# Key and value biases written by ACT instead of multiplied in by PE, in a fused attention and FP4 layer

## The reference

```
q, k = elu(x @ Wq + bq) + 1, elu(x @ Wk + bk) + 1      # 16 heads of 16 columns
v    = x @ Wv + bv
k    = k / sqrt(sum(k*k per head) + 1e-6)
attn = (q @ k^T) @ v                                    # no softmax, no mask
y    = layernorm(x + attn @ Wo + bo) * gamma + beta     # eps 1e-6
x1   = layernorm(x + y)                                 # eps 1e-5
out  = layernorm(x1 + ffn(x1))                          # silu(gate) * up, then down
```

## Time and profile before

| | before |
|---|---|
| median of 3 runs | 707.12 us (707.09 to 709.07) |
| profiled execution: its time | 708.65 us |
| profiled execution: span | 706.9 us |
| mean granted clock of PE | 0.994 |
| PE busy | 687.4 us, 97% |
| DVE busy | 593.9 us, 84% |
| ACT busy | 485.0 us, 69% |
| POOL busy | 611.9 us, 87% |
| PE's share of the chain that ended last | 89% |
| bias products (L401) | 64 instructions, 18.1 us busy by their own lengths, which overlap |

### The profile page before, as it was taken

The page is one execution under the profiler, slowest core; times in us unless marked ns, Lnnn a source line. Parts: engine busy times, 40 slices in busy tenths (PEclk is TensorE's granted clock), DMA queues, the critical chain, the costliest instruction groups (busy, mean ns, idle before and its releaser), DMA issues.

```text
span 706.9 us, 14230 instructions
## 1 busy us (share of the span) xinstructions
PE 687.4 (97%) x4370; PEld 603.9 (85%) x4370; DVE 593.9 (84%) x1448; ACT 485.0 (69%) x943; POOL 611.9 (87%) x951
## 2 busy tenths in 40 slices
PE   7999999999988999999999999999999999999995
PEld 6887878778866799999999999999999999999995
DVE  5788888885878888898898898998998898998774
ACT  4666766766667767767767767767767767767664
POOL 2989888987998999988988988988988988989766
PEclk9999999999999999999999999999999999999999
DMA  9443343344322021111111111111111111100001
GB/s 280 170 136 134 128 135 123 113 165 152 118 91 90 30 62 45 61 46 46 56 65 46 60 46 46 53 68 46 61 46 46 52 69 46 60 17 16 16 32 45
DMA packets 22272, 55.05 MB, mean 78 GB/s; under 512 B 2547, under 2 KB 5557, under 8 KB 22197
## 3 DMA queue, kind: packets, MB, share of 16 engines
q1 hardware_dynamic: 21776, 54.01, 22.5%
q10 hardware_dynamic: 420, 0.13, 0.1%
HBM read 28.90 MB, written 25.17 MB: 76 GB/s over the span
## 4 chain that ended last, share of the span: by engine, by line
PE 89%; POOL 4%; issue 3%; DVE 2%; ACT 1%; DMA 1%; SPq 0%; POOLq 0%; DVEq 0%; ACTq 0%
PE banks L377 23%; PE banks L379 22%; PE banks L378 22%; PE banks L519 8%; PE banks L490 7%; PE banks L415 2%; PE banks L388 2%; PE banks L533 1%; PE banks L532 1%; PE banks L401 1%; PE banks L444 1%; DMA arena<-in_L_attn_x_dram 1%; POOL arena L1126 1%; PE banks L452 1%; POOL lnbuf L1111 0%
## 5 line engine op out<-in xcount | busy, mean ns | idle before, releaser
L377 PE MATMUL banks<-wgu_hi,actT_lo 128*128 128x512 f32 (+1 forms) x384 | 149.8, 390 | 1.6 <-DVE resid L790 1.3
L378 PE MATMUL banks<-wgu_lo,actT_hi 128*128 128x512 f32 (+1 forms) x384 | 144.0, 375 | 0.0
L379 PE MATMUL banks<-wgu_hi,actT_hi 128*128 128x512 f32 (+1 forms) x384 | 143.3, 373 | 0.0
L1126 POOL TENSOR_TENSOR arena<-arena 128x960 f32<-128x960 f16 (+2 forms) x68 | 115.1, 1693 | 0.0
L688 ACT ACTIVATE arena<-banks 128x512 f32<-128x512 f32 x64 | 38.4, 599 | 111.7 <-PE banks L379 111.5
L1102 POOL TENSOR_TENSOR arena<-arena 128x704 f32<-128x704 f32 x64 | 89.1, 1392 | 21.1 <-DVE arena L907 19.0
L377 PE MATMUL banks<-wd_hi,actT_lo 128*128 128x256 f32 x320 | 100.1, 313 | 0.0
L920 DVE TENSOR_TENSOR actT_lo<-banks,actT_hi 128x512 fp32r<-128x512 f32 (+1 forms) x132 | 85.6, 674 | 16.9 <-ACT actT_hi L674 16.2
L379 PE MATMUL banks<-wd_hi,actT_hi 128*128 128x256 f32 x320 | 90.3, 282 | 0.0
L378 PE MATMUL banks<-wd_lo,actT_hi 128*128 128x256 f32 x320 | 90.2, 282 | 0.0
L377 PEld LDWEIGHTS banks<-wgu_hi,actT_lo 128*128 128x128 f32 x384 | 72.5, 189 | 11.2 <-DVE resid L790 1.7
(11 more groups left out here) (126 smaller groups left out, 1932.8 us busy)
## 6 DMA issues: line engine op xcount, KB each, us to landing
xs<-x_plus_scratch SPq DMA_DIRECT2D x32, 512.0 KB, 3.3
x_plus_scratch<-xs SPq DMA_DIRECT2D x24, 512.0 KB, 2.9
arena<-in_L_attn_x_dram SPq DMA_DIRECT2D x32, 256.0 KB, 3.6
out_dram<-arena SPq DMA_DIRECT2D x32, 256.0 KB, 2.1
x_plus_scratch<-arena SPq DMA_DIRECT2D x8, 512.0 KB, 2.9
resid<-in_L_ffn_w_down_dram SPq DMA_DIRECT2D x1, 704.0 KB, 7.7
resid<-in_L_ffn_w_gate_dram SPq DMA_DIRECT2D x1, 640.0 KB, 8.1
resid<-in_L_ffn_w_up_dram SPq DMA_DIRECT2D x1, 640.0 KB, 9.5
```

The costliest lines, as they stand in the source:

```text
L377: nc.tensor.matmul(dst, sl, mh, start=(k == 0), stop=False, skip_group_check=shared)
L378: nc.tensor.matmul(dst, sh, ml, start=False, stop=False, skip_group_check=shared)
L379: last = nc.tensor.matmul(dst, sh, mh, start=False, stop=(ended and k == n - 1), skip_group_check=shared)
L1126: nc.gpsimd.tensor_tensor(blocks(va[:, (n + 1) % 2, a:b]), blocks(vqc[n % 2].bitcast(F16)[:, a:b]), each(s14[:, n % 2, a // BLK:b // BLK]) ...
```

## The change

ACT gets a new operation, `kv_biases(p)`: before kv_project(p) it copies one row that holds bk + 1 and bv (broadcast over 128 partitions, 512 columns) into both banks of pair p, for p = 2 to 23 (`filled`). The products of these pairs add onto it (`begun`, so the first has start=False), the bias product L401 is left out, and DVE's v_bias becomes a copy. It stands in ACT's step p-1, behind x_high (and kv_out_copy) and before k_seeds. PE waits for it before kv_project. Pairs 0, 1 and 24 to 31 stay as they are. The row needs one more load (bk, 128 KB, on SP's queue before the loads of pairs 2 and 3), once on ACT an addition of 1, and a tile of its own for bo.

The addition of the half in the rounding of weights goes from DVE (w_round) to ACT (w_f16_chunk), 11 times.

In the steps p of 4 to 23 that have no turns of weights and for which (p-2) mod 4 is over 0, kv_accumulate(p-2) moves from behind kv_project(p) to in front of it, right behind the turns of x. These are nine: 4, 5, 7, 11, 15, 17, 19, 20 and 21.

```diff
@@ -123,7 +124,8 @@
         vqb = [words(o, RN * (RW + 2) // 2).bitcast(U16).rearrange("p (r c) -> p r c", c=RW + 2) for o in (7808, 8303)]
 
         qr = words(9075, 512)
-        bv_b, bo_b = words(9587, D), words(9843, D)
+        bkv = words(9587, 2 * D)
+        bv_b = bkv[:, D:2 * D]
         vqc = [words(o, VW // 2) for o in (8947, 9587)]
 
         qe = words(10099, 512)
...
@@ -265,6 +268,10 @@
 
             return p - 1 if p <= MERGE else p
 
+        def filled(p):
+
+            return 2 <= p < MERGE
+
         def mo_bank(b):
             return Q_BANK if b < B - 1 else KV_BANK + 1
 
@@ -314,6 +321,7 @@
             sp.dma_start(wq_st, Wq.rearrange("(k p) n -> p k n", p=P)).then_inc(wq_in, 16)
             sp.dma_start(bo_b[:, :], bo.partition_broadcast(P)).then_inc(xb_in, 16)
             sp.dma_start(beta_b[:, :], beta.partition_broadcast(P)).then_inc(xb_in, 16)
+            sp.dma_start(bkv[:, 0:D], bk.partition_broadcast(P)).then_inc(bk_in, 16)
@@ -370,11 +378,11 @@
 
         @block.tensor
         def _(pe):
-            def split_product(dst, stat, mov, n, ended=True, shared=False):
+            def split_product(dst, stat, mov, n, begun=False, ended=True, shared=False):
 
                 for k in range(n):
                     (sh, sl), (mh, ml) = stat(k), mov(k)
-                    nc.tensor.matmul(dst, sl, mh, start=(k == 0), stop=False, skip_group_check=shared)
+                    nc.tensor.matmul(dst, sl, mh, start=(not begun and k == 0), stop=False, skip_group_check=shared)
                     nc.tensor.matmul(dst, sh, ml, start=False, stop=False, skip_group_check=shared)
                     last = nc.tensor.matmul(dst, sh, mh, start=False, stop=(ended and k == n - 1), skip_group_check=shared)
                 return last
@@ -393,13 +401,17 @@
                 pe.wait_ge(xT_lo_s, p + 1)
                 after(pe, k_feat, kv_read(p))
                 after(pe, v_s, kv_read(p))
+                if filled(p):
+                    pe.wait_ge(kv_bias, p - 1)
                 for jj in range(2):
                     bank = kv_banks(p) + jj
                     c = slice((p % PPB) * 2 * P + jj * P, (p % PPB) * 2 * P + (jj + 1) * P)
-                    split_product(ps[:, bank, :], lambda k: (xT_hi[:, k, c], xT_lo[:, k, c]),
-                                  lambda k: (wkv_hi[:, k, :], wkv_lo[:, k, :]), KT, ended=False, shared=True)
-                    last = nc.tensor.matmul(ps[:, bank, 0:D], rows[:, D:], rows[:, 0:D], start=False, stop=True,
-                                            skip_group_check=True)
+                    last = split_product(ps[:, bank, :], lambda k: (xT_hi[:, k, c], xT_lo[:, k, c]),
+                                         lambda k: (wkv_hi[:, k, :], wkv_lo[:, k, :]), KT, begun=filled(p), ended=filled(p),
+                                         shared=True)
+                    if not filled(p):
+                        last = nc.tensor.matmul(ps[:, bank, 0:D], rows[:, D:], rows[:, 0:D], start=False, stop=True,
+                                                skip_group_check=True)
                 last.then_inc(kv_ps, 1)
 
             def kv_accumulate(p):
@@ -457,6 +469,11 @@
                     if p - 1 in WG_STEP:
                         pe.wait_ge(wT_lo, WG_STEP[p - 1] + 1)
                     x_transpose(p + 1)
+
+
+                early = 4 <= p < MERGE and p not in WG_STEP and (p - 2) % PPB > 0
+                if early:
+                    kv_accumulate(p - 2)
                 if p == -1:
                     warm_up(6)
                 if p == 0:
@@ -467,7 +484,7 @@
                 if p in WG_STEP:
                     pe.wait_ge(xT_lo_s, p + 2)
                     weights_turn(WG_STEP[p])
-                if pair(p - 2):
+                if pair(p - 2) and not early:
                     kv_accumulate(p - 2)
                 if p == 1:
                     pe.wait_ge(watt_lo, 3)
@@ -579,6 +596,9 @@
                 act.wait_ge(w_scaled, c + 1)
                 after(act, w_deq, c - 1)
                 nc.scalar.activation(wqn[:, c % 2, :], halves(wy[:, c % 2, :]), ACT.Copy, scale=F16_ONE).then_inc(w_f16, 1)
+                act.wait_ge(w_f16, c + 1)
+                q = wqn[:, c % 2, :].bitcast(U16)
+                nc.scalar.activation(q, q, ACT.Copy, bias=ROUND_HALF).then_inc(w_half, 1)
 
             def weights_high(g):
                 act.wait_ge(wT_ps, g + 1)
@@ -606,6 +626,19 @@
                 after(act, k_feat, p)
                 b = kv_banks(p)
                 nc.scalar.activation(kexp, ps[:, b:b + 2, 0:D], ACT.Exp, bias=mone[:, :]).then_inc(k_exp, 1)
+
+            def kv_biases(p):
+
+                if p == 2:
+                    act.wait_ge(bk_in, 16)
+                    act.wait_ge(bv_in, 16)
+                    nc.scalar.activation(bkv[:, 0:D], bkv[:, 0:D], ACT.Copy, bias=1.0).then_inc(bk_one, 1)
+                    act.wait_ge(bk_one, 1)
+                act.wait_ge(k_feat, p - 1)
+                act.wait_ge(v_s, p - 1)
+                b = kv_banks(p)
+                nc.scalar.activation(ps[:, b:b + 2, :], bkv[:, :].unsqueeze(1).broadcast_to([P, 2, 2 * D]),
+                                     ACT.Copy).then_inc(kv_bias, 1)
 
             def k_squares(p):
                 act.wait_ge(k_feat, p + 1)
@@ -636,6 +669,8 @@
                     act.wait_ge(cols_set, 2)
                 if p >= 7 and (p - 7) % PPB == 0 and (p - 7) // PPB < B:
                     kv_out_copy((p - 7) // PPB)
+                if filled(p + 1):
+                    kv_biases(p + 1)
                 if pair(p - 1):
                     k_seeds(p - 1)
                 if pair(p - 2):
@@ -771,9 +806,7 @@
                 scales_of(wam[:, g], wsn[:, g], ws14[:, g], winv[:, g], w_nudged, w_scale_s, c + 1)
 
             def w_round(c):
-                dve.wait_ge(w_f16, c + 1)
                 q = wqn[:, c % 2, :].bitcast(U16)
-                nc.vector.tensor_scalar(q, q, ROUND_HALF, None, ALU.add).then_inc(w_half, 1)
                 dve.wait_ge(w_half, c + 1)
                 nc.vector.tensor_scalar(q, q, ROUND_MASK, None, ALU.bitwise_and).then_inc(w_rounded, 1)
 
@@ -803,8 +836,11 @@
             def v_bias(p):
                 after(dve, kv_acc, p - 2)
                 b = kv_banks(p)
-                nc.vector.tensor_tensor(vb[:, p % 3, :, :], ps[:, b:b + 2, D:2 * D],
-                                        bv_b[:, :].unsqueeze(1).broadcast_to([P, 2, D]), ALU.add).then_inc(v_s, 1)
+                if filled(p):
+                    nc.vector.tensor_copy(vb[:, p % 3, :, :], ps[:, b:b + 2, D:2 * D]).then_inc(v_s, 1)
+                else:
+                    nc.vector.tensor_tensor(vb[:, p % 3, :, :], ps[:, b:b + 2, D:2 * D],
+                                            bv_b[:, :].unsqueeze(1).broadcast_to([P, 2, D]), ALU.add).then_inc(v_s, 1)
 
             def k_sums(p):
                 dve.wait_ge(k_sq, p + 1)
```

More of the change, by code:

```diff
@@ L76, in build @@
         gamma_b = sb("gamma_b", [P, D])
+        bo_b = sb("bo_b", [P, D])
         bq_c, bq_neg, bq_one = (sb(n, [P, KT]) for n in ("bq_c", "bq_neg", "bq_one"))
@@ L173, in build @@
         G_BANK, U_BANK, GU_BANK, T_BANK, AT_BANK, DN_BANK = 6, 7, 0, 4, 2, (3, 1)
-        wk_in, wv_in, wq_in, wffn_in, rows_in, bv_in, bq_in, xb_in, late_in = (
-            sem(n) for n in ("wk_in", "wv_in", "wq_in", "wffn_in", "rows_in", "bv_in", "bq_in", "xb_in", "late_in"))
+        wk_in, wv_in, wq_in, wffn_in, rows_in, bv_in, bq_in, bk_in, xb_in, late_in = (
+            sem(n) for n in ("wk_in", "wv_in", "wq_in", "wffn_in", "rows_in", "bv_in", "bq_in", "bk_in", "xb_in", "late_in"))
         consts_set, small_set, cols_set, mask_s = sem("consts_set"), sem("small_set"), sem("cols_set"), sem("mask")
@@ L186, in build @@
         xT_ps, xT_hi_s, xT_lo_s = sem("xT_ps"), sem("xT_hi_done"), sem("xT_lo_done")
+        bk_one, kv_bias = sem("bk_one"), sem("kv_bias")
         kv_ps, k_exp, k_feat, v_s, k_sq, k_ssq, k_se, k_log, k_seed = (
```

## The result

The change makes the kernel slower: median 712.74 us (710.76 to 713.65, six runs) against 707.19 (706.96 to 709.07, six runs) for before, ratio 1.0067 with a 95% interval of 1.0053 to 1.0081. 705.7 was forecast, and the range ended at 709.0. The profiled execution took 712.61 us with a span of 710.7 and a mean granted clock of 0.996, against 708.65, 706.9 and 0.994: 4.0 us more, because the profile of before lay 1.5 over its median.

A forecast was written before the change was run, and what follows sets the result against it. PE was taken as the bound, with ACT and POOL limiting gains. Of 5.3 us off PE's list, 1.2 at the step 22 turn plus step 23's 0.24 remained: 707.12 - 1.4 = 705.7 us, range 702.7 to 709.0.

The forecast's parts named there:

- The bias products: On PE, 22 pairs: two products fewer each, 44 x 0.12 = 5.3 us off PE's list, the most to win.
- The write's own price: On ACT, one 1024-element write into two banks per step: 1.06 us, 0.96 of queue, bounds 0.90 and 1.27.
- rival B: ACT becomes the pacemaker in steps 2 to 22 if a write holds its queue 1.3: 709.5 us, chance 0.15.
- The start: First steps: newton(0) at 18.0 instead of 17.01, k_hat(2) and k_hat(3) 1.0 later.
- The early waits: PE waits for k_hat before the moved kv_accumulate: 0.8, 0.2, 0.5 in steps 4, 5, 7, about 1.3 in step 21.
- The early block: kv_accumulate ahead of kv_project in nine steps: the move itself wins 0, ends -0.3 and +1.8.
- the neighbour: A float32 block next to kv_accumulate might remove its 0.20 extra cost, 9 x 0.20 = 1.8; taken as 0.
- The step that failed: Weight turns in steps 8, 12, 16: DVE off the path otherwise, x_low(p+1) makes PE wait 0.3, 0.1, 0.1.
- Steps 8 to 18 win 11 x 0.24 = 2.6 less 0.5 of waits: PE's sum over these steps, from 0.1 late at step 8 to step 19 beginning 2.0 early.
- The forecast gain of 1.4: Whole kernel: the step 22 weight turn 1.2 earlier, held by POOL, and 0.24 from step 23; chance 0.45.
- The probability of 0.13 for slower: Chance of a measurement over 709.2 us, mostly from ACT becoming the pacemaker through a costlier write.
- the rivals: PE keeps most of its gain, chance 0.22; ACT becomes the pacemaker, 0.15; nothing reaches the end, 0.18.

The follow-up runs named there:

- e3: The changed kernel with key and value biases left out in pairs 2 to 23 (no ACT write, no PE product): ratio to before 0.9963.
- e12: The changed kernel with the write between k_exps and k_squares, from pair 3 on, and the last four weight turns one step later: ratio to before 0.9932.
- e4: The kernel before with only the nine kv_accumulate moved in front of kv_project: ratio to before 1.0005.
- e1: The changed kernel with kv_accumulate back behind kv_project in the nine steps: ratio to before 1.0065.
- e2: The changed kernel with the bias write moved behind k_seeds, ahead of q_maps and k_exps: ratio to before 1.0077.
- e14: The changed kernel with the bias write moved between q_maps and k_exps: ratio to before 1.0074.
- e5: The changed kernel with the bias write moved into ACT's wait between k_exps and k_squares: ratio to before 0.9970, median 706.54 us.
- e8: The changed kernel with the write between k_exps and k_squares, kv_accumulate back behind kv_project and the half back on DVE: ratio to before 0.9990.
- e9: The changed kernel with the half back on DVE: ratio to before 1.0060.
- e11: The changed kernel with the write between k_exps and k_squares and the last four weight turns one step later: ratio to before 0.9949.

## Why the prediction was wrong, step by step

**The bias products, right.** 44 products at 0.12; the product is left in 20 rows instead of 64, steps without a wait are 0.24 to 0.34 shorter, and in e3 and e12 they stay so.

**The write's own price, right.** 1.06 forecast and 0.96 of queue; 1027 ns and 0.95 (80.47 to 81.42). That closes rival B: its direction came, but its price of 1.3 a write did not.

**The start, nearly right.** newton(0) forecast at 18.0; 18.47, of which 0.44 is the clock's rise ahead of step 1. The early waits: 0.8, 0.2, 0.5 and 1.3 forecast for steps 4, 5, 7 and 21; measured 0.73, 0.21, 0 and 1.07. Step 7 had none because step 6 had already stopped PE for 1.17. That stop I did not forecast: kv_accumulate of step 6 waits for DVE's mask_heads, behind an x_low that ACT's late x_high had pushed:

```profile
45.43 0.69 PE L427 MATMUL banks<-arena 128*64 128x64 f32 x16 [1.12 <-DVE arena L865]
```

**The early block, right in what the neighbour gives, incomplete in what it costs.** 0 was taken for the neighbour; with the change a step is 0.02 to 0.03 shorter for it (5.36 early, 5.39 late), in e4 up to 0.05 longer. But the prediction charged the block only with waits for k_hat. e4 shows a further 1.3 us of length through a later k_exps, and after against e1, step 22 left out, 1.3 for both kinds together.

**The step that failed** is the one that priced the write's effect in steps 8, 12 and 16: "DVE is off the path but for the weight turn ... I expect waits of 0.3, 0.1, 0.1", and with it the sum "Steps 8 to 18 win 11 x 0.24 = 2.6 less 0.5 of waits". The waits were 1.13 three times, and 0.46 twice in steps 9 and 13, 4.3 in all for a forecast of 0.5; with the 0.85 of step 18 it was 5.2, and instead of winning 2.1 in steps 8 to 18 PE lost 2.3. I had asked of these turns only when x_low was ready. I had said two paragraphs earlier that every seed is 0.96 later and that POOL runs on from the seed, but carried this on only to the places where PE already waited in the trace (step 4, step 21, the turn at 142.40). At 80.85 PE showed no wait, and I read that as slack; there was none, for the 0.10 behind w_deq's end is the distance that a waiting PE has too. And I had costed ACT as a sum of busy time per four steps, 23.6 against 23.63, where the answer lay in the order: k_exps, at 3.64 after the step's start, already stood as late as the end of a step with a turn allows (2.65 behind it), so each 0.1 that it moved could cost 0.1 of PE. After shows the chain over w_deq, e2 and e14 that the chain over k_exps alone costs as much, and e5 that neither costs PE more than in before when the write stands behind k_exps.

**What follows from it.** Step 19 began 3.40 late instead of 2.0 early, newton(18) started at 127.52 instead of 122.1, the turn in step 22 at 146.40 instead of 141:

```profile
127.52 0.25 POOL L1072 TENSOR_TENSOR arena<-arena 128x32 f32<-128x32 f32 x1 [2.12 <-ACT arena L613]
```

The forecast gain of 1.4 there had rested on PE's lead, which did not exist. That a lead passes on to the end was right in its form, but what passed on was the lag: 3.99 at step 23, 3.8 at the end. The probability of 0.13 for slower had come only from the write's price; the mechanism that came true was in none of the rivals.

## What to carry to other kernels

When work is moved to an engine with time to spare, price it by what stands behind it in that engine's queue: follow every later instruction to the places where the full engine needs its result, and compare the two times there, also where the trace shows no wait, for two that arrive together leave none. The time to spare of a queue is where it waits: the same 1.03 us write cost 5.6 us more in one place than in another, six or seven instructions further on. And where a wait names a releaser that ended long before (82.48 for a start at 83.47), look among the other things the instruction waits for, for one that ended just before it.

## What the runs showed of the hardware that was not expected

**An idle in step 22 was followed by half clock in three versions.** PE stood idle ahead of the weights' turn in step 22 in every version that turns them there. e1, PE, and the stretches ahead and behind (from:to, length, busy of PE, PEld, DVE, ACT, POOL, then the granted clock):

```profile
144.53 0.63 PE L464 MATMUL banks<-ident,resid 128*128 128x128 f32 x4 [2.84 <-issue]
```

```profile
141.30:144.50 3.20, 0.39 (x2) 0.00 (x0) 1.50 (x5) 3.17 (x8) 3.20 (x5) 1.00 0.26 102
146.20:149.60 3.40, 3.40 (x10) 2.61 (x9) 1.92 (x4) 1.24 (x3) 3.40 (x4) 0.50 0.00 1
```

A granted clock of 0.50 is the level of 1.2 GHz; products then start 0.43 apart (146.74, 147.17) instead of 0.23. e8 has the same 3.4 us after an idle of 2.27, and e3 after one of 1.57. After, with 1.63, kept 1.00:

```profile
146.40 0.63 PE L464 MATMUL banks<-ident,resid 128*128 128x128 f32 x4 [1.63 <-issue]
```

```profile
146.40:149.90 3.50, 3.50 (x30) 2.88 (x31) 3.32 (x6) 2.83 (x6) 3.17 (x7) 1.00 0.41 124
```

The length of the idle alone does not decide it. In step 22 idles of 2.84, 2.27 and 1.57 were followed by half clock, those of 1.61 (e2), 1.63, 1.64 (e14), 1.65 (e9) and 1.37 (e5) were not, nor was one of 1.82 in step 6 of e2. Between 198 and 208 us an idle of 2.56 to 2.76 ends in each of the 14 versions: in 11 of them half clock followed, in e4, e5 and e14 the clock stayed at 1.00 until after another idle of about 2.5, 12 us later. What decides stays open. By estimate 3.4 us at half clock do 1.7 us of work: a lead of PE ahead of a fixed wait can turn into a loss. That is part of why step 22 took 11.34, 10.09 and 10.66 in e1, e3 and e8 against 8.51 in after. Turning the weights one step later takes the idle itself away: 6.70 in e11 against 8.50 in e5.

**DVE's 16-bit mask took 0.19 to 1.25 us for one shape.** The mean of the same instruction in before and after:

```profile
L778 DVE TENSOR_SCALAR arena<-arena 128x384 uint16<-128x384 uint16 x11 | 8.5, 770 | 0.4
```

```profile
L811 DVE TENSOR_SCALAR arena<-arena 128x384 uint16<-128x384 uint16 x10 | 9.0, 895 | 0.0
```

It is 895 in after, 490 in e2 and 461 in e5. In after one ran from 80.73 to 81.88, while POOL's addition of 512 columns ran from 80.46 to 81.76; in e2 one that started at 81.40, 0.07 before POOL's addition ended, took 0.25, and POOL's next operation 0.93 instead of 0.86. It looks as if the two engines took turns, so that taking one of DVE's two operations away gave back less than its length; no kernel tested that by itself, and it isn't shown.
